# Two PSUM banks in turns for the projections, two for the experts, and the down projection a slot later

## The reference

```python
# gated linear attention: 8 heads, key width 128, value width 64
q, k, v = xn @ Wq, (xn @ Wk) * 128 ** -0.5, xn @ Wv
alpha = sigmoid((xn @ Wg + bg) / 16)                 # one decay for each token and head
state = alpha * state + k[..., None] * v             # over the tokens, one after the other
attention = (q . state) * sigmoid(xn @ Wog) @ Wo
# mixture of experts: 64 experts, 8 of them for each token, 256 places in each
scores = sigmoid(xn @ gate_w.T)                      # best 4 of 8 groups, then best 8 experts
y_e = (silu(x_e @ w_gate_e) * (x_e @ w_up_e)) @ w_down_e      # x_e: the up to 256 rows of expert e
out[token] += 2.5 * weight * y_e                     # scattered back to the tokens
result = x + attention + out
```

## Time and profile before

| What | us |
|---|---|
| Median of three runs | 1408.48 |
| The profiled execution | 1409.67 |
| Its span, from the first to the last instruction | 1408.0 |
| TensorE busy with matmuls | 1304.0 |
| VectorE busy | 957.4 |
| ScalarE busy | 550.2 |
| GpSimd busy | 524.0 |

### The profile page before, as it was taken

How to read it: one execution, slowest core, us unless ns; L and a number is a source line. 1 busy time by engine, 2 the same in 40 slices (tenths; PEclk the granted TensorE clock), 3 DMA queues, 4 the chain that set the end, 5 groups by cost and what they waited for, 6 DMA issues and landing times.

```text
span 1408.0 us, 27621 instructions
## 1 busy us (share of the span) xinstructions
PE 1304.0 (93%) x9460; PEld 1131.9 (80%) x9460; DVE 957.4 (68%) x2427; ACT 550.2 (39%) x1078; POOL 524.0 (37%) x405
## 2 busy tenths in 40 slices
PE   4899999999999999899999999999999999999981
PEld 3788788888888877788888888888888888888871
DVE  4787878788886658667566575775757757667450
ACT  5655645555554422233333233333333333333220
POOL 1010100100100067446357364563654636636521
PEclk9899999999999999999999999999999999999996
DMA  6466534353531311246467465664655747646676
GB/s 214 125 230 204 172 103 159 114 174 110 181 116 64 106 60 44 90 132 161 109 166 163 124 156 123 155 147 125 157 146 137 166 106 177 159 123 156 162 239 209
DMA packets 134369, 202.96 MB, mean 144 GB/s; under 512 B 12384, under 2 KB 106144, under 8 KB 134176
## 3 DMA queue, kind: packets, MB, share of 16 engines
q1 hardware_dynamic: 108064, 160.57, 35.9%
q0 software_dynamic: 26240, 41.63, 15.7%
HBM read 152.81 MB, written 57.74 MB: 150 GB/s over the span
## 4 chain that ended last, share of the span: by engine, by line
PE 70%; DVE 11%; DMA 7%; issue 6%; ACT 3%; SPq 2%; DVEq 0%; POOLq 0%; POOL 0%; ACTq 0%
PE bank L668 18%; PE bank L745 6%; PE bank L789 6%; PE bank L765 6%; PE bank L680 5%; PE bank L712 4%; PE bank L730 4%; PE bank L694 4%; PE bank L733 3%; PE bank L798 3%; DMA arena<-in_L_ffn_w_down_dram 3%; PE bank L703 3%; DMA out_dram<-arena 3%; PE bank L615 2%; PE bank L779 2%
## 5 line engine op out<-in xcount | busy, mean ns | idle before, releaser
L538 POOL DMA_INDIRECT arena<-table,idx_all x132 | 167.6, 1270 | 269.8 <-DVE arena L1366 222.4
L546 POOL DMA_INDIRECT acc<-arena,idx_all x128 | 225.5, 1762 | 81.8 <-DMA acc<-arena,idx_all 47.2
L668 PE MATMUL bank<-xp,wq 128*128 128x512 f32 x768 | 209.5, 408 | 0.0
L668 PE MATMUL bank<-xp,wk 128*128 128x512 f32 x768 | 202.9, 399 | 0.0
L668 PEld LDWEIGHTS bank<-xp,wk 128*128 128x128 f32 x768 | 139.0, 188 | 30.9
L668 PEld LDWEIGHTS bank<-xp,wq 128*128 128x128 f32 x768 | 137.0, 190 | 25.2
L1263 DVE TENSOR_TENSOR_SCAN Dt<-decay,eye_b 128x512 f32<-128x512 f32 x128 | 155.4, 1216 | 2.0 <-DMA decay<-decay_dram 2.0
L712 PE MATMUL bank<-qT,kT 128*128 128x128 f32 x1024 | 136.0, 276 | 2.7 <-ACT kT L963 2.7
L745 PEld LDWEIGHTS bank<-V,kw 128*128 128x128 f32 x960 | 120.0, 191 | 14.9 <-issue 10.4
L712 PEld LDWEIGHTS bank<-qT,kT 128*128 128x128 f32 x1024 | 124.4, 192 | 5.0 <-ACT kT L963 4.5
L745 PE MATMUL bank<-V,kw 128*128 128x64 f32 x960 | 127.1, 275 | 0.0
(11 more groups left out here) (153 smaller groups left out, 2241.0 us busy)
## 6 DMA issues: line engine op xcount, KB each, us to landing
decay<-decay_dram SPq DMA_DIRECT2D x64, 512.0 KB, 5.8
carry<-decay_dram SPq DMA_DIRECT2D x60, 512.0 KB, 4.7
arena<-in_L_attn_x_dram SPq DMA_DIRECT2D x16, 512.0 KB, 4.8
table<-arena SPq DMA_DIRECT2D x16, 512.0 KB, 2.9
xT_dram<-arena SPq DMA_DIRECT2D x16, 512.0 KB, 3.0
arena<-in_L_ffn_w_gate_dram SPq DMA_DIRECT2D x64, 128.0 KB, 2.7
arena<-in_L_ffn_w_up_dram SPq DMA_DIRECT2D x64, 128.0 KB, 3.0
arena<-in_L_ffn_w_down_dram SPq DMA_DIRECT2D x64, 128.0 KB, 3.5
```

Of the source, the lines that this page charges most:

```text
L538: pool.indirect_dma_start(out=xg[:, e % 2, j, :], out_offset=None, in_=table[:, :], in_offset=bass.IndirectOffsetOnAxis(ap=idx_all[:, e, j ...
L546: pool.indirect_dma_start(out=acc[:, :], out_offset=bass.IndirectOffsetOnAxis(ap=idx_all[:, e, j:j + 1], axis=0), in_=yb[:, e % 2, j, :], ...
L668: last = mm(bank[which][:, :], w[:, part, k, h * DK:(h + 1) * DK], xp[:, other, k, :], start=(k + i == 0), stop=(k == KD - 1 and i == 2))
```

## The change

The projections of list, expert and last steps share banks 0 and 1 in turns, in the order of the program, each waiting for the copy of the projection two turns back. Bank 4 becomes the second bank of the experts (and of the pairs in the list step): odd experts use it, even ones bank 7. The tokens of e wait for `y_cp` of e - 2 alone. The down projection of an expert moves from the end of its slot to the next slot, right behind the tokens of the next expert; the one of a step's last expert goes into the head of the next step, ahead of the fourth value projection. The hidden product moves from place 1 to place 2, behind the key projection. VectorE reads the output behind `tokens_low_e`, and in odd slots scales the queries ahead of the hidden products. In the list step, slots 2, 4 and 6 hold five pairs, slot 8 holds one and slot 7 no output gate (it moves to slot 8). The first expert step stands outside the loop. SyncE's and GpSimd's programs are the same.

```diff
+PAIR_AT = [(s, place) for s in range(1, H) for place in ((0, 1, 2, 4, 3) if s in (2, 4, 6) else (0, 1, 2, 3))]
+PAIR_AT += [(H, 0)]
...
+        turns = [("v", 0), ("q", 0), ("v", 1), ("k", 0), ("v", 2), ("v", 3)]
+        for h in range(1, H + 1):
+            turns += [("q", h)] if h < H else []
+            turns += [("og", og_slots("experts").index(h))] if h in og_slots("experts") else []
+            turns += [("k", h)] if h < H else []
+
+        def bank_of(kind, what, i):
+            if in_turns(kind):
+                return bank[turns.index((what, i)) % 2]
+            return bank[{"q": 0, "k": 1, "v": 4, "og": 4}[what]]
+
+        def bank_free(eng, c, kind, what, i):
+            n = turns.index((what, i)) - 2
+            if n < 0:
+                eng.wait_ge((qk_cp, og_cp)[n + 2], (16 * c, 4 * c)[n + 2])
+                return
...
+        expert_bank = (bank[7], bank[4])
...
             def slot_pair(n):
-                wait_past(pe, tok_cnt, n)
+                wait_past(pe, tok_cnt, n - 1)
...
             def expert_tokens(c, j):
                 pe.wait_ge(gathered[j % 2], ((c - E0) * (STEP_E // 2) + j // 2 + 1) * 16 * NHALF)
-                if j > 0:
-                    pe.wait_ge(y_cp, e)
-                else:
-                    pe.wait_ge(kw_cp, at(c, 8, 1))
+                if not isinstance(e, int) or e > 1:
+                    pe.wait_ge(y_cp, e - 1)
...
-                if kind == "slots" and s > 0:
-                    slot_pair(SLOTS_S // 2 * (s - 1) + place)
-                if kind == "experts" and s > 0 and place != 2:
-                    {0: expert_tokens, 1: expert_hidden, 3: expert_down}[place](c, s - 1)
+                if kind == "slots" and (s, place) in PAIR_AT:
+                    slot_pair(PAIR_AT.index((s, place)))
+                if kind == "experts" and s > 0 and place == 0:
+                    expert_tokens(c, s - 1)
+                    if s > 1:
+                        expert_down(c, s - 2)
+                if kind == "experts" and s > 0 and place == 2:
+                    expert_hidden(c, s - 1)
...
                 scores(c, 0)
-                proj_v(c, 3)
+                if kind in ("experts", "last") and not (isinstance(c, int) and c == E0):
+                    expert_down(c - 1, STEP_E - 1)
+                proj_v(c, kind, 3)
```

and in VectorE's program:

```diff
                     if place == 0:
-                        tokens_low_e(c, s - 1)
+                        if s > 1:
+                            tokens_low_e(c, s - 1)
+                            expert_out(c, s - 2)
                     if place == 2:
                         expert_hidden(c, s - 1)
                         if s < H:
                             weights_low_e(c, s)
-                    if place == 3:
-                        expert_out(c, s - 1)
...
                     scores_decayed(c, s - 1)
+                    if s == 1 and kind in ("experts", "last") and not (isinstance(c, int) and c == E0):
+                        expert_out(c - 1, STEP_E - 1)
+                    if s == 1 and kind == "experts":
+                        weights_low_e(c, 0)
                     if s == 1 and not is_first(c) and not is_last(c):
                         projected(c, 2, kind)
+                        if kind == "experts":
+                            tokens_low_e(c, 0)
                         projected(c, 3, kind)
...
+                    if s % 2 and kind in ("experts", "last"):
+                        queries_scaled(c, s // 2)
                     beside(c, kind, s, 2)
-                    if s % 2 and not is_first(c):
+                    if s % 2 and not is_first(c) and kind not in ("experts", "last"):
                         queries_scaled(c, s // 2)
```

More of the change, by code:

```diff
@@ L301, in is_first, with in_turns @@
             return isinstance(c, int) and c == 0
+        def in_turns(kind):
+            return kind in ("slots", "experts", "last")
         def og_slots(kind):
-            return (1, 3, 5, 8) if kind in ("experts", "last") else (1, 3, 5, 7)
+            return (1, 3, 5, 8) if in_turns(kind) else (1, 3, 5, 7)
+        turns = [("v", 0), ("q", 0), ("v", 1), ("k", 0), ("v", 2), ("v", 3)]
[12 more added lines that the diff above has]
+                return
+            before, k = turns[n]
+            if before == "v":
+                eng.wait_ge(v_cp, 4 * c + k + 1)
+            elif before == "og":
+                eng.wait_ge(og_cp, 4 * c + k + 1)
+            else:
+                eng.wait_ge(qk_cp, at(c, 16, 2 * k + (before == "k") + 1))
+        expert_bank = (bank[7], bank[4])
         def is_last(c):
@@ L693, in proj_og @@
                     for i, (part, other) in enumerate(PARTS):
-                        last = mm(bank[4][:, :], wog[:, part, k, j * P:(j + 1) * P], xp[:, other, k, :],
+                        last = mm(to[:, :], wog[:, part, k, j * P:(j + 1) * P], xp[:, other, k, :],
                                   start=(k + i == 0), stop=(k == KD - 1 and i == 2))
@@ L778, in expert_tokens @@
                         lo = k * CAP + half * P
-                        last = tr(bank[7][:, lo:lo + P], xg[:, j % 2, half, k * P:(k + 1) * P], ident[:, :])
+                        last = tr(expert_bank[j % 2][:, lo:lo + P], xg[:, j % 2, half, k * P:(k + 1) * P], ident[:, :])
                 last.then_inc(xg_ps, 1)
@@ L877, in _ @@
             step(S_SLOTS, "slots")
-            with pe.Fori(E0, E1) as c:
+            step(E0, "experts")
+            with pe.Fori(E0 + 1, E1) as c:
                 step(c, "experts")
@@ L1065, in _ @@
             step(S_SLOTS, "slots")
-            with act.Fori(E0, E1) as c:
+            step(E0, "experts")
+            with act.Fori(E0 + 1, E1) as c:
                 step(c, "experts")
@@ L1411, in beside @@
                     keep_firsts()
-                if kind == "slots" and s > 0:
-                    n = SLOTS_S // 2 * (s - 1) + place
+                if kind == "slots" and (s, place) in PAIR_AT:
+                    n = PAIR_AT.index((s, place))
                     count_pair(n)
@@ L1446, in step @@
                         ends_kept(c, s // 2)
-                    if s == 1 and kind == "experts":
-                        beside(c, kind, 0, 3)
                     early = kind in ("slots", "experts")
@@ L1481, in _ @@
             step(S_SLOTS, "slots")
-            with dve.Fori(E0, E1) as c:
+            step(E0, "experts")
+            with dve.Fori(E0 + 1, E1) as c:
                 step(c, "experts")
```

126 lines of the change are left out of this document (67 added, 59 removed).

## The result

The changed kernel takes **1381.6 us** (median of 4 runs, 1380.72 to 1384.49) where the kernel before takes 1407.7 (median of 4 on the same chip, 1406.92 to 1409.47): a ratio of 0.9817, 95% interval 0.9801 to 0.9832. The profiled execution took 1381.22 us, its span 1379.6. Forecast were 1396 us and a range of 1379 to 1412. The sign and the range hold; the gain is 26 us where 12.4 were worked out.

A forecast was written before the change was run, and what follows sets the result against it. TensorE, busy 93% of the span, was taken to bound it, with waits on VectorE in the list step and SyncE's queue bounding the last. -9 + 0 - 8 + 4.6 = -12.4 us on 1409.67 gave 1397.3, as median 1396; range 1379 to 1412.

The forecast's parts named there:

- The list step: With two banks and new places for the pairs, VectorE becomes the bound and the list step shortens by 9 us.
- the sum of VectorE's work: List step, slots 1 to 7: VectorE's instructions add up to 62 us, against 59 for TensorE.
- The projections on two banks: List, expert and last steps: projections taking turns on two banks wait for no late copy, so cost nothing.
- the rival with +19: Projections in turns on two banks wait for ScalarE's copies, at most +19 us over eight expert steps; chance 0.05.
- The expert steps: Eight expert steps: old waits of 28 us go, new waits for gathers come, leaving a gain of 8 us.
- The waits of the earlier trace: Expert steps: TensorE's waits of 3.5 us a step, for tokens' low part and output reads among others, all go.
- The new wait: Expert steps: tokens wait for a late gather, 0.43 us in slots 3 and 5, 1.83 in slot 7, 2.7 a step.
- the gather is in time: Rival: in expert steps gathers land early enough, so these give -26 us and the kernel takes 1378; chance 0.2.
- The tail: Last step: the last expert's down projection in its head delays scatters and stores, costing 4.6 us, from +2 to +8.
- The gather loop: Rival: in expert steps each late gather landing lengthens a ring of dependent work, +26 us, 1430 in all; chance 0.2.

The follow-up runs named there:

- e7: The changed kernel with the list step's 32 slot products at their old places, four in each of slots 1 to 8, still on two banks: ratio 0.9823.
- e1: The changed kernel with VectorE's decay scan of expert slots 3, 5 and 7 moved behind the scaling of the queries, beside the gathers: ratio 0.9859.
- e3: The changed kernel with the down projection and output of each step's last expert put back to the end of its own slot 8: ratio 0.9772.
- e5: The changed kernel with VectorE's lists and scan in list-step slot 8 moved behind the next step's low part of tokens, gated outputs and state: ratio 0.9768.
- f1: The changed kernel with old slot-product places on two banks, the last expert's down projection home, and lists and scan late in list-step slot 8: 1376.26 us, ratio 0.9755.
- e8: The changed kernel with the list step's slot products at their new places but all on one bank, each waiting for the previous count: ratio 0.9928.

## Why the prediction was off, step by step

**The list step** (-9, measured -6.5). The eighth slot did get shorter: 8.9 us from its keys to the next step where it was 11.9 and should have been near 6. The chain on VectorE behind the last count of slot 7 is 5.84 us long (forecast 5.8). But this count ended 81.65 us into the step (571.65), and the sum of VectorE's work had put it at 76.8; I had allowed 2.4 us for gaps where there were 4.9. That is the term which was too good. TensorE in that slot:

```profile
568.32 0.38 PE L685 MATMUL bank<-arena,sel_all 64*128 64x128 bf16 x4 [0.97 <-DVE arena L1289]
...
574.29 1.10 PE L785 MATMUL bank<-V,kw 128*128 128x64 f32 x8
577.49 1.66 PE L717 MATMUL bank<-wv,xp 128*128 128x512 f32 x6 [2.10 <-DVE xp L1236]
```

The part that I left out is GpSimd, whose comparisons run without a gap for 36.8 and then 20.7 us and twice hold up TensorE (0.7 and 0.6 us):

```profile
509.82 36.82 POOL L592 TENSOR_SCALAR sel_all<-arena 64x256 bf16<-64x256 bf16 x36 [8.22 <-PE bank L685]
547.02 20.74 POOL L592 TENSOR_SCALAR sel_all<-arena 64x256 bf16<-64x256 bf16 x20 [0.38 <-PE bank L685]
```

And e7 shows that the rest is the new places, which I had taken for the source of the gain. With the products at their old places the step gives 9.5 us. That this is about my number is luck: I had got it from places that cost time, and 2.9 us of it are matmuls that became shorter, at a granted clock of 1.00 in place of 0.96.

**The projections on two banks** (0, right). No row of TensorE waits for a copy between 577 and 1279 us, so the rival with +19 is out.

**The expert steps** (-8, measured -26): the step that failed. The waits of the earlier trace rows went as worked out. The new wait was put at 2.7 us a step, 1.83 in slot 7 and 0.43 in slots 3 and 5; it is 0.8 (6.2 us over eight steps), nearly all in slot 7. The mis-sized term is the landing of the gather: 3.9 us taken from the median of before, 3.0 measured between the second gather and the tokens. With the output's 0.2 us it makes up the 1.2 us of slot 7 and all of slots 3 and 5. The wait came out 1.9 us a step below the forecast, 15 of the 18 us. Of the other 3 us most lies in the first expert step, and I did not look for its source.

I had read that median as a property of the transfer. It was a mixture: 3.8 us for held gathers of even places, 3.0 to 3.6 for the unheld ones beside them, 6.2 at place 1, and 4.35 at places 3, 5 and 7, which left 3.65 us behind a 512 KB load. The changed kernel's gathers at these places are held by 0.1 us at most (1.17 us), those of before were not, and they leave 6.0 us behind that load; they land after 3.1. The prediction had seen that the gathers "now leave after the 512 KB loads that stood beside them", and gave it 0.35 us a step, while the sum went on with a landing that contained those loads. What the loads cost and what the scan 0.14 us into a gather cost at these places, no run separates. e1 shows what a held gather costs here: 0.6 us of landing, and 7.6 us over the expert steps.

The rival "the gather is in time" had this very term at 3.0 us and came nearest (-26, 1378) with a chance of 0.2; the least landing of 3.0 us stood in the same line as the median that I chose. Its hit is in part luck, since the bound worked out from landings of 3.0 us alone was -19.

**The tail** (+4.6, measured +3.4). SyncE sees all scatters landed 22.3 us into the step (forecast 22.5), and the first store of an added result goes out at 34.5 (forecast 33.2, 27.2 before). SyncE's queue, start and us:

```profile
1301.79 0.38 SPq L397 DMA_DIRECT2D addend<-acc  x1
...
1313.96 0.41 SPq L493 DMA_DIRECT2D out_dram<-arena  x1
```

The mechanism and its size are right, and e3 shows that it could be had for nothing: 4.5 us come back.

**Rivals on the other side.** The gather loop did not slow the step. The one long wait, 1.79 us at 1009.55, is no late landing: GpSimd issued that gather 1.75 us behind the output in place of 0.86, with no wait that the profile shows, and does so at this gather in e1, e3, e5, e7 and f1 too; the pair landed after 3.4 and 3.0 us.

## What to carry to other kernels

A duration or landing taken from the profile of before holds only as long as what ran beside it stays. Take it from the very instructions on which the forecast's wait rests, not from the median of all, and ask what stood beside them, on the other engines and in the DMA queue, and whether the change keeps that neighbour. If it does not, the least value is the better guess. When work is put a slot later to take a wait away, leave the last one of a step where it was, if what follows the step needs it. And a new placing of products deserves a run apart from the second bank that makes it possible: here the old places made the list step 3 us shorter in e7, and 1 us in f1 against e5.

## What the runs showed of the hardware

A gather (128 rows, indirect DMA on GpSimd) whose issue takes 1.06 us alone takes longer when a VectorE instruction with both inputs in SBUF is running as it starts; it ends 0.86 to 0.96 us after that instruction, be it the scan or the product of `carry` and `qT`. So it takes 1.17 us where the scan has 0.27 us left and 1.88 where it has 1.02. An instruction with one input in PSUM does not hold it (1.09).

A gather that is not held lands 3.0 to 3.1 us after its start at the quickest places. 3.65 us behind the issue of a 512 KB load it took 4.3 to 4.4 at places 5 and 7, 4.5 us behind it 3.7 to 3.8, and 6.0 us behind it 3.1; that the loads are the cause is read from the order and not tested.

TensorE's granted clock fell in the list steps that have idle times of 1 to 2 us: 0.96 over the step before, 0.90 in e8, 0.63 for the 4.6 us behind one wait of 1.71 us in f1, yet 1.00 in e7 behind a wait as long. Of its two levels the full one is 2.4 GHz and the other 1.2; groups of four matmuls in f1 took 0.64 us instead of 0.39. Part of what the change gained in the list step, 2.6 of 6.5 us, is this clock.

In the expert steps VectorE's gated outputs start 0.05 us after the end of TensorE's outputs in slots 2, 4 and 6 of the changed kernel, and 0.4 to 0.8 us after it in e7 and e8, of whose text only the list step differs. I did not find out why.
